# A token-mixing, attention and expert tower: rebuilt prologue and epilogue

## Chip, cores and metric

The kernel runs on one core of a Trainium2 chip. The metric is the device time of one execution in microseconds (us).

## What is computed

The input is x of 64 samples, 128 rows and 192 values. The reference, cut to what matters:

```python
def tok(x):                                   # per sample: 128 channels, 64 x 3 pixels
    h = layernorm(x.reshape(b, t, 192), ln0_g, ln0_b)
    h = relu(conv2d(h, conv1_w, conv1_b, ((2, 2), (1, 1))))       # 5 x 3 taps, 128 -> 128
    h = layernorm(h, ln0_g, ln0_b)
    h = relu(conv2d(h, conv2_w, conv2_b, ((2, 2), (0, 0))))       # 5 x 2 taps, 128 -> 128
    h = layernorm(h, ln1_g, ln1_b)
    h = relu(conv2d(h, conv3_w, conv3_b, ((2, 2), (0, 0))))       # 5 x 2 taps, 128 -> 256
    res = layernorm(concat(two halves), ln1_g, ln1_b)
    return res @ out_w + out_b                                    # 128 tokens of width 64
def attn(x):
    q, vf, vb = split(x @ wqv_w.T + wqv_b)                        # 8 heads of width 64
    a = -sum_w |q[s] - k[t]| / 8, k = x * wk                      # L1 distance, all pairs of tokens
    a = softmax(concat(a, 0), axis=s)[:t]
    o = sum over heads of (a @ vf + a.T @ vb)
    return x + (o * sigmoid(1.702 * o)) @ fanin_w.T + fanin_b
def ffn(x):                                   # one expert of 32 for each token
    idx = argmax(x @ router_w.T + router_b)
    return relu(relu(x @ W1[idx] + b1[idx]) @ W2[idx] + b2[idx])
h = tok(x); h = h + attn(norm(h)); h = h + ffn(norm(h))
```

## The kernel before

The work goes by pairs of samples, 32 pairs in all. For each pair there are four stages: `tok` (the three convolutions and their layer norms), `norm` and `kq` (the norm ahead of attention, the keys `kT` and the queries `qparts`), the 128 **units** with `attend`, and `experts`. A unit is one head with 16 query tokens of one sample: TensorE makes the differences q - k of all its pairs in PSUM with four bf16 matmuls (line 403), and one engine takes the absolute value and adds. For a unit that is not *shared* VectorE does both in one reduction (line 805, about 1.2 us). For a *shared* unit ScalarE writes the absolute values to `absd` (line 601, about 1.0 us), then a DMA adds the two halves of a group of two to four units (line 1061), GpSimd adds three more levels (lines 1072 to 1079), and VectorE finishes with a short reduction (line 816). The table `SHARED` (line 45) says for each of the 16 groups of 8 slots which heads are shared. The unit in slot s uses place s mod 3 of the PSUM tensor `psU`, so TensorE waits for the reader of slot s - 3.

All engines run the same list of 128 slots for each pair, each engine its own part, and each engine carries out its instructions in the order in which they are written. The tables `AT_AT`, `EX_AT`, `NORM_AT`, `KQ_AT` and `TOK_AT` (lines 126 to 135) say at which slot a step is written. Iteration i holds the units of pair i, the second half of `attend` and the `experts` of pair i - 1, `norm` and `kq` of pair i + 1 and `tok` of pair i + 2. So the **prologue** must do `tok` of pairs 0 and 1 and `norm` and `kq` of pair 0 before the first unit, and the **epilogue** has the second half of `attend` and the `experts` of the last pair, for which no other work is left.

In the prologue SP issues the loads in one row: x of pair 0, the list `first` (`ident`, `ln0g`, `ln0b`, `w1`, `b1`), then `weights`, `parts_of` and at last x of pair 1. All engines wait for the whole of `first`, and from the second layer on for the whole of the rest (semaphore `loaded`; VectorE waits for it at the slot of conv1, lines 1018 to 1020, and then runs `weigh`, which makes the table `pattern` from the key weights). Then all engines go through 256 slots with pair 0 at slot s and pair 1 at s - 40:

```python
for s in range(2 * SLOTS):
    tok(0, s, psL, lead_pe, lead_act, lead_dve)
    norm(0, s - SLOTS)
    kq(0, 0, s - SLOTS - QUERY_AFTER)      # QUERY_AFTER = 66
    tok(1, s - LEAD)                       # LEAD = 40
```

SP then loads `flat` from `pattern` (four DMAs of 768 KB) and, once `qpart3` is made, from the queries; unit 0 waits for these and for `kT`. The convolutions and most small matmuls are in f32 and appear in the trace as two records each. In the epilogue every step of `attend` and `experts` goes through the one PSUM bank `psZ`: `turna` and `turnb` (the attention weights transposed, four heads each), `pv` (eight matmuls), `fan`, `turn`, `route`, `turnoh`, `hida`, `hidb` (the experts' hidden layer in two halves) and `out`, each of which waits until the one before has been read.

Of the kernel before, what the change touches and what calls it, by code (L numbers as in the profile page):

```python
# [25 lines left out]
T = 128  # L26
J = 64
# [28 lines left out]
LEAD = 40  # L56
QUERY_AFTER = 66
# [7 lines left out]
def group_ends(slot):  # L65

    return 0 <= slot < SLOTS and slot % HEADS == SHARED[slot // HEADS][-1]
# [69 lines left out]

def vit_tower(nc, a, out):
    PAIRS = a["x"].shape[0] // 2
    x_v = a["x"].rearrange("b t f -> t b f")  # L140
    out_v = out.rearrange("b t w -> t b w")

    with ExitStack() as ctx:  # L143
# [3 lines left out]
        def sem(name):  # L147
# [30 lines left out]
        one = sb("one", [T, 1])  # L178

# [62 lines left out]
        loaded_first = sem("loaded_first")  # L242
        loaded = sem("loaded")
        ready = sem("ready")
        filled = sem("filled")
# [22 lines left out]
        first = [(ident, a["ident"]), (ln0g, a["ln0g"]), (ln0b, a["ln0b"]), (w1, a["w1"]), (b1, a["b1"])]  # L268
        weights = [
            (w2, a["w2"]), (b2, a["b2"]), (ln1g, a["ln1g"]), (ln1b, a["ln1b"]), (w3, a["w3"]), (b3, a["b3"]),  # L270
            (ln1g_col, a["ln1g_col"]), (ln1b_col, a["ln1b_col"]), (wout, a["wout"]), (bout, a["bout"]),
            (wk, a["wk"]), (rank, a["rank"]), (we2, a["we2"]),
# [5 lines left out]
        READY = 18  # L278
        FIRST = 16 * len(first)
# [15 lines left out]
        def _(sp):  # L295
            sp.dma_start(xin[:, :, :], x_v[:, 0:2, :]).then_inc(x_in, 16)
            for dst, src in first:
                sp.dma_start(dst[:], src).then_inc(loaded_first, 16)
            for dst, src in weights:
                sp.dma_start(dst[:], src).then_inc(loaded, 16)  # L300
            sp.wait_ge(zeroed, 1)
            for dst, src in parts_of:
                sp.dma_start(dst, src).then_inc(loaded, 16)
# [20 lines left out]
            def prologue():  # L324
                load_x(1)
                load_x(2)
                sp.wait_ge(pattern_made, 14)
# [36 lines left out]
        def _(pe):  # L364
# [8 lines left out]
            def unit(i, slot):  # L373
# [21 lines left out]
                if isinstance(j, int) and j < 0:  # L395
                    pass
                elif shared(before):
                    pe.wait_ge(a_abs, A_PAIR * j + A_BEFORE[before + 1])
                else:
                    pe.wait_ge(d_done, D_PAIR * j + D_BEFORE[before + 1])  # L400
# [76 lines left out]
            def attend(p, b, slot):  # L477
# [11 lines left out]
                for n, name in enumerate(("turna", "turnb")):  # L489
                    for m in spread(slot, AT_AT[name], AT_AT["turn_len"], 4):  # L490
                        if m == 0:
                            take_bank(at_act, AT_ACT.after(g, ("turneda", "turnedb")[n]))
                            pe.wait_ge(at_act, AT_ACT.after(g, ("scale3", "scale7")[n]))
                        mm = nc.tensor.transpose(psZ[:, m * T:m * T + T], P[:, 4 * n + m, 0, :], ident[:, :])
# [12 lines left out]
            def experts(p, slot):  # L507
# [23 lines left out]
                for n, name in enumerate(("hida", "hidb")):  # L531
                    for m in spread(slot, EX_AT[name], EX_AT["hid_len"], 2):
                        if m == 0:
                            take_bank(ex_act, EX_ACT.after(p, ("relua", "relub")[n]))
                        q = 2 * n + m
                        mm = nc.tensor.matmul(psZ[:, m * 256:m * 256 + 256], we1[:, q * T:q * T + T], xa[:, :],  # L536
# [3 lines left out]
                for q in spread(slot, EX_AT["out"], EX_AT["out_len"], 5):  # L540
                    if q == 0:
                        take_bank(ex_act, EX_ACT.after(p, "relu"))
                    mm = nc.tensor.matmul(psZ[0:LAT, 0:256], be2[:, :] if q == 4 else we2[:, q, :],  # L543
# [8 lines left out]
            def prologue():  # L552
                pe.wait_ge(loaded_first, FIRST)
                pe.wait_ge(ready, READY)
                for s in range(2 * SLOTS):
                    if s == TOK_AT["conv2"]:
                        pe.wait_ge(loaded, LOADED)
                    tok(0, s, psL, lead_pe, lead_act, lead_dve)
                    norm(0, s - SLOTS)
                    kq(0, 0, s - SLOTS - QUERY_AFTER)  # L560
                    tok(1, s - LEAD)

            def iteration(i, late=True, tokens=True, ahead=True):
# [3 lines left out]
                for s in range(SLOTS):  # L567
# [23 lines left out]
        def _(act):  # L591
            def unit(i, slot):
                if not shared(slot):
                    return
                c = slot // HEADS
                u = SHARED[c].index(slot % HEADS)
# [100 lines left out]
            def attend(p, b, slot):  # L697
# [6 lines left out]
                for n in spread(slot, AT_AT["exp"], AT_AT["exp_len"], HEADS):  # L704
                    if n == 0:

                        act.wait_ge(d_done, D_PAIR * p + D_BEFORE[64 * (b + 1)])
                        act.wait_ge(a_done, TREES * p + CHUNKS * (b + 1))
# [7 lines left out]
                for n, name in enumerate(("turna", "turnb")):  # L716
                    if slot == AT_AT[name] + AT_AT["turn_len"]:
                        act.wait_ge(at_pe, AT_PE.after(g, name))
                        nc.scalar.activation(P[:, 4 * n:4 * n + 4, 1, :],  # L719
                                             psZ[:, :].rearrange("p (h t) -> p h t", h=4), ACT.Copy).then_inc(at_act, 1)  # L720
# [11 lines left out]
            def experts(p, slot):  # L732
# [501 lines left out]
```

## Time and profile before

| | |
|---|---|
| three runs | 3576.53, 3578.32, 3587.60 us; median 3578.32 us |
| profiled execution | 3586.24 us, of which the span from first to last instruction 3584.1 us |
| busy in the span | TensorE matmuls 3276.2 us (91%), VectorE 3115.8 (87%), GpSimd 2851.3 (80%), ScalarE 2694.5 (75%) |
| first unit starts | 82.8 us |
| last units end | 3534.5 us |
| the softmax of the last half pair starts | 3547.1 us |
| mean granted TensorE clock | 0.983 |

"Span" is read from the profile's first line; the rest of the profiled time (2.1 us) lies outside it. A window row gives for each engine its busy time and its count of instructions in a stretch. A timeline row gives start, duration, engine, line, operation, output and inputs, and in brackets how long the engine was idle before it and what it waited for.

### The profile page before, as it was taken

How to read it: one execution, taken by the hardware profiler on the slowest of the kernel's cores; microseconds unless marked ns; L12 is line 12 of the kernel's file. 1: busy time of each engine (PE TensorE's matmuls, PEld its weight loads, DVE VectorE, ACT ScalarE, POOL GpSimd, SP SyncE). 2: the span in 40 equal slices, each digit the busy share in tenths (PEclk: the TensorE clock that was granted, in tenths of full speed). 3: DMA queues.
4: the chain of work that ended last, by engine and by line, in shares of the span. 5: the costliest groups of instructions: out<-in, count | busy, mean ns of one | idle time of the engine just before them, and what ended most of it. 6: DMA issues, size and time to landing. Idle time of an engine off the chain costs nothing. (4 is left out here: it accounts for less than half of the span.)

```text
span 3584.1 us, 78481 instructions
## 1 busy us (share of the span) xinstructions
PE 3276.2 (91%) x23008; PEld 2420.3 (68%) x23008; DVE 3115.8 (87%) x4449; ACT 2694.5 (75%) x4801; POOL 2851.3 (80%) x2724
## 2 busy tenths in 40 slices
PE   5899999999999999999999999999999999999886
PEld 4666667666667766667666677666677666677554
DVE  3889988898898898888899899899899899898884
ACT  1777877777877777777777777777777777777774
POOL 1788888888888888878888888888888888888874
PEclk8999999999999999999999999999999999999998
DMA  3777877787777787777887777787877787777874
GB/s 94 154 157 153 161 151 154 150 165 154 156 153 156 153 162 156 155 148 151 158 160 155 157 153 154 157 158 155 159 153 155 156 158 155 155 153 152 160 157 82
DMA packets 198692, 545.31 MB, mean 152 GB/s; under 512 B 68054, under 2 KB 132438, under 8 KB 145272
## 3 DMA queue, kind: packets, MB, share of 16 engines
q0 software_dynamic: 73728, 503.35, 71.0%
q1 hardware_dynamic: 124920, 41.40, 5.9%
q8 instruction: 24, 0.39, 0.0%
q14 instruction: 20, 0.16, 0.0%
HBM read 10.79 MB, written 2.10 MB: 4 GB/s over the span
## 5 line engine op out<-in xcount | busy, mean ns | idle before, releaser
L805 DVE TENSOR_REDUCE S<-psU 128x16 f32<-128x1024 f32 x2176 | 2603.5, 1217 | 295.7 <-PE psU L403 288.4
L403 PE MATMUL psU<-flat,kT 99*128 99x256 bf16 x16384 | 2315.7, 275 | 230.5 <-ACT absd L601 106.6
L601 ACT ACTIVATE absd<-psU 128x1024 f32<-128x1024 f32 x1920 | 1957.8, 1023 | 627.0 <-PE psU L403 604.7
L403 PEld LDWEIGHTS psU<-flat,kT 99*128 99x128 bf16 x16384 | 1489.2, 98 | 915.2 <-DVE S L805 235.7
L1072 POOL TENSOR_TENSOR absd<-absd 128x1024 f32<-128x1024 f32 (+2 forms) x512 | 1182.1, 2309 | 195.3 <-DMA absd<-absd 194.3
L1061 POOL DMA_DIRECT2D absd<-absd x512 | 453.9, 886 | 297.6 <-ACT absd L601 254.5
L1076 POOL TENSOR_TENSOR absd<-absd 128x512 f32<-128x512 f32 (+2 forms) x512 | 611.0, 1193 | 40.2
L1079 POOL TENSOR_TENSOR absd<-absd 128x256 f32<-128x256 f32 (+2 forms) x512 | 352.4, 688 | 40.1
L415 PE MATMUL psC<-c1in,w 128*128 128x384 f32 (+1 forms) x930 | 315.1, 421 | 0.6
L501 PE MATMUL psZ<-P,v 128*128 128x256 f32 x1024 | 311.2, 386 | 0.8 <-ACT P L719 0.8
L434 PE MATMUL psC<-c3in,w 128*128 128x128 f32 x1240 | 255.6, 289 | 4.5 <-DVE c3in L847 4.2
L816 DVE TENSOR_REDUCE S<-absd 128x64 f32<-128x256 f32 (+2 forms) x512 | 201.5, 393 | 34.8 <-POOL absd L1079 33.0
L434 PEld LDWEIGHTS psC<-c3in,w 128*128 128x128 f32 x1240 | 195.6, 193 | 37.0 <-issue 25.6
L423 PE MATMUL psC<-c2in,w 128*128 128x256 f32 x620 | 186.6, 383 | 1.5 <-DVE c2in L847 1.5
L715 ACT ACTIVATE P<-P,rden 128x128 f32<-128x128 f32 x512 | 175.0, 393 | 0.3 <-DVE rden L919 0.3
L501 PEld LDWEIGHTS psZ<-P,v 128*128 128x128 f32 x1024 | 156.1, 192 | 16.6 <-ACT P L719 7.8
L710 ACT ACTIVATE P<-S 128x129 f32<-128x129 f32 x512 | 152.9, 305 | 10.6 <-DVE S L816 10.6
L415 PEld LDWEIGHTS psC<-c1in,w 128*128 128x128 f32 x930 | 141.7, 191 | 9.9 <-DVE c1in L847 4.3
L485 PE MATMUL psZ<-wqv,x1T_late 65*128 65x256 f32 x512 | 135.0, 386 | 0.7 <-ACT v L702 0.7
L1138 POOL TENSOR_TENSOR qparts<-qrest,qparts 128x512 bf16<-128x512 f32 x64 | 83.5, 1304 | 25.3 <-ACT qparts L695 25.3
L710 ACT ACTIVATION_READ_ACCUMULATOR P<-S 128x1 f32 x512 | 99.8, 195 | 0.0
L423 PEld LDWEIGHTS psC<-c2in,w 128*128 128x128 f32 x620 | 93.7, 190 | 5.5 <-DVE c2in L847 2.0
(166 smaller groups left out, 2187.0 us busy)
## 6 DMA issues: line engine op xcount, KB each, us to landing
absd<-absd POOLq DMA_DIRECT2D x416, 1024.0 KB, 7.8
flat<-qparts SPq DMA_DIRECT2D x3072, 8.0 KB, 4.0
absd<-absd POOLq DMA_DIRECT2D x64, 768.0 KB, 6.5
absd<-absd POOLq DMA_DIRECT2D x32, 512.0 KB, 4.8
xin<-in_x SPq DMA_DIRECT2D x32, 192.0 KB, 7.9
flat<-pattern SPq DMA_DIRECT2D x4, 768.0 KB, 10.8
out_h<-result SPq DMA_DIRECT2D x32, 64.0 KB, 5.9
w<-in_w SPq DMA_DIRECT2D x1, 1280.0 KB
```

The costliest lines, as they stand in the source:

```text
L403: mm = nc.tensor.matmul(psU[:, slot % PLACES, m], kT[0:ROWS + 3, b, m, :], flat[0:ROWS + 3, half % HALVES, :, lo:lo + BLOCK], start=True, ...
L415: mm = nc.tensor.matmul(o_v[:, :, :, o:o + wn], w1[:, 3 * dy + dx, :], c1in[:, :, dy:dy + J, w0:w0 + wn], start=(n == 0), stop=(n == 14))
L423: mm = nc.tensor.matmul(z[:, 0:4 * J].rearrange("p (b j w) -> p b j w", b=2, w=2), w2[:, n, :], c2in[:, :, dy:dy + J, dx:dx + 2], start=(n ...
L434: mm = nc.tensor.matmul(z[:, 0:2 * T].rearrange("p (b a j) -> p b a j", b=2, a=2)[:, :, hf, :], w3[:, m, hf * T:hf * T + T], c3in[:, :, dy ...
L501: mm = nc.tensor.matmul(psZ[:, 0:2 * T], v[:, n, :, :].rearrange("p a w -> p (a w)"), P[:, n, :, :].rearrange("p a t -> p (a t)"), start=( ...
L601: nc.scalar.activation(absd[:, c % GROUPS, :, u], psU[:, slot % PLACES].rearrange("p (n a) s w -> p n (a s w)", n=2), ACT.Abs).then_inc(a_ ...
L710: nc.scalar.activation(P[:, n, :, :].rearrange("p a t -> p (a t)")[:, 0:T + 1], S[:, b, n, :], ACT.Exp, scale=-1.0 / 8.0, accum_out=den[:, ...
L805: nc.vector.tensor_reduce(S[:, b, hd, SB * c:SB * c + SB], psU[:, slot % PLACES].rearrange("p a s w -> p s a w"), AX.XY, ALU.add, apply_ab ...
L1061: nc.gpsimd.dma_start(absd[:, c % GROUPS, 0, 0:n], absd[:, c % GROUPS, 1, 0:n], accum_op=ALU.add) \
L1072: nc.gpsimd.tensor_tensor(lo, lo, hi, ALU.add).then_inc(a_tree, 1)
L1076: nc.gpsimd.tensor_tensor(lo, lo, hi, ALU.add).then_inc(a_tree, 1)
L1079: nc.gpsimd.tensor_tensor(lo, lo, hi, ALU.add).then_inc(a_tree, 1)
```

## The change

- **Loads.** `first` is cut into `for_norm` (`ln0g`, `ln0b`), `for_conv1` (`w1`, `b1`) and `for_keys` (`ident`, `wk`), with a semaphore each; then x of pair 1, then `for_conv2`, then the rest. Each step waits for its own part only.
- **Constants.** Those that the first layer doesn't need are set behind the first layer norm (semaphore `ones`); four small ones go to GpSimd. ScalarE runs a one-column Copy at the start. `weigh` is cut in two, `split_keys` and `weigh`, and put behind pair 0's first and second layer norm.
- **Order.** The two loops of 256 slots give way to `lead_in`: a table of how far pair 0 and pair 1 have got at each step. Pair 0's queries are made in the middle of pair 1's conv3, its keys behind pair 1's last layer norm; pair 1's last three slots are written in slot 0 of iteration 0 (`lead_out`).
- **Matmuls on zeros.** 44 bf16 matmuls of 256 columns at the start (`WARM`), and in the epilogue 50, 16, 31, 9, 14 and 2 ahead of `turna`, `fan`, `turn`, `route`, `turnoh` and `hida` (`STILL`). Their output is overwritten or not read.
- **Last pair.** `SHARED_LAST` takes the place of `SHARED` in the last four groups of the last pair: 9 shared units there in place of 15. `turnb` and `hidb` go to the bank `psC`, so that `pv` can begin when the first four heads are ready and `hidb` need not wait for the reader of `hida`.

```diff
+SHARED_LAST = {12: (1, 5), 13: (2, 4, 6), 14: (1, 5), 15: (0, 2)}
...
+LEAD_IN = [(43, 31), (46, 31), (48, 36), (59, 36), (63, 37), (73, 49), (75, 50), (76, 51), (77, 54), (116, 74),
+           (117, 74), (127, 78), (128, 89), (128, 92)]
+LEAD_LAST = (95, 118, 125)
+LEAD_TAIL = 1
+WEIGH = (2, 3)
+WARM = 44
+
+def lead_in(first, second, norm, kq, between=None):
+    n, k = NORM_AT, KQ_AT
+    now = [0, 0]
+    def run(job, *slots):
+        for x in dict.fromkeys(slots):
+            job(x)
+    def run_to(row, first_to, second_to):
+        run(first, *range(now[0], first_to))
+        run(second, *range(now[1], second_to))
+        now[:] = first_to, second_to
+        if between:
+            between(row)
+    for row, (first_to, second_to) in enumerate(LEAD_IN):
+        run_to(row, first_to, second_to)
+    run(norm, n["stat"], n["rstd"], n["x"])
+    run_to(-1, SLOTS, LEAD_LAST[0])
+    run(norm, n["turn"], n["turn"] + 1)
+    run(kq, *range(k["q"], k["q"] + max(k["q_len"], 1)), k["qpart1"], k["qrest1"], k["qpart2"], k["qpart3"])
+    run_to(-1, SLOTS, LEAD_LAST[1])
+    run(norm, n["part1"], n["rest1"], n["part2"], n["part3"], n["hx"])
+    run(kq, k["kT"], k["kT"] + 1)
+    run_to(-1, SLOTS, LEAD_LAST[2])
+
+def lead_out(second, slot):
+    for x in spread(slot, 0, LEAD_TAIL, SLOTS - LEAD_LAST[2]):
+        second(LEAD_LAST[2] + x)
+
+STILL = dict(turna=50, fan=16, turn=31, route=9, turnoh=14, hida=2)
...
+        for_norm = [(ln0g, a["ln0g"]), (ln0b, a["ln0b"])]
+        for_conv1 = [(w1, a["w1"]), (b1, a["b1"])]
+        for_keys = [(ident, a["ident"]), (wk, a["wk"])]
+        for_conv2 = [(w2, a["w2"]), (b2, a["b2"]), (ln1g, a["ln1g"]), (ln1b, a["ln1b"])]
...
# TensorE
             def prologue():
-                pe.wait_ge(loaded_first, FIRST)
-                pe.wait_ge(ready, READY)
-                for s in range(2 * SLOTS):
+                pe.wait_ge(stilled, 1)
+                for n in range(WARM):
+                    nc.tensor.matmul(psU[:, 0, 0], still[:, 0:T], still[:, :], start=True, stop=True)
...
+            def stay_awake(n):
+                for _ in range(n):
+                    nc.tensor.matmul(psU[:, 125 % PLACES, 0], still[:, 0:T], still[:, :], start=True, stop=True)
             def epilogue():
+                pe.wait_ge(d_done, d_before(PAIRS - 1, 126))
                 for s in range(SLOTS):
-                    attend(PAIRS - 1, 1, s)
-                    experts(PAIRS - 1, s)
+                    for name, n in STILL.items():
+                        if s == (EX_AT[name] if name in EX_AT else AT_AT[name]):
+                            stay_awake(n)
+                    attend(PAIRS - 1, 1, s, psC)
+                    experts(PAIRS - 1, s, psC)
...
# TensorE, pv: the second four heads wait for turnb's copy on their own
+                        pe.wait_ge(at_act, AT_ACT.after(g, "turnedb" if other is None else "turneda"))
+                    if n == HEADS // 2 and other is not None:
                         pe.wait_ge(at_act, AT_ACT.after(g, "turnedb"))
...
# ScalarE
             def prologue():
+                act.wait_ge(stilled, 1)
+                nc.scalar.activation(still_act[:, :], still[:, 0:1], ACT.Copy).then_inc(stilled, 1)
...
# VectorE
+                def between(row):
+                    if row == WEIGH[0]:
+                        split_keys()
+                    if row == WEIGH[1]:
+                        weigh()
...
# every engine, iteration 0 only
+                    if not late:
+                        lead_out(lambda x: tok(1, x), s)
```

## Rows read from the trace of the kernel before

**Rows 1.** Windows, instructions of line 415: busy (count) of PE, PEld; clock; DMA share; GB/s.

```profile
14.70:18.10 3.40, 3.39 (x7) 2.43 (x8) 1.00 0.99 206
18.10:25.00 6.90, 6.86 (x24) 4.58 (x23) 1.00 0.30 71
```

**Rows 2.** Timeline of the prologue's first layer, all engines.

```profile
9.44 0.23 DVE L980 CAST ident_b<-ident 128x128 bf16<-128x128 f32 x1 [3.37 <-DMA b<-in_b]
...
11.03 0.49 ACT L610 ACTIVATE psU<-xin 128x384 f32<-128x384 f32 x1
...
14.71 10.26 PE L415 MATMUL psU<-c1in,w 128*128 128x384 f32 x30 [14.71 <-DVE c1in L847]
...
22.18 0.18 DVE L984 TENSOR_REDUCE pick<-ident 96x1 f32<-96x32 f32 x1 [7.62 <-DMA be<-in_be]
...
31.33 5.94 PE L423 MATMUL psU<-c2in,w 128*128 128x256 f32 x14 [6.37 <-DVE c2in L847]
```

**Rows 3.** Timeline: from one convolution to the next, and conv3's pace.

```profile
47.33 0.56 ACT L614 ACTIVATE psC<-psC,b 128x384 f32<-128x384 f32 x1 [6.70 <-PE psC L415]
...
50.87 1.13 PE L423 MATMUL psC<-c2in,w 128*128 128x256 f32 x4 [1.49 <-DVE c2in L847]
...
63.83 3.36 PE L434 MATMUL psC<-c3in,w 128*128 128x128 f32 x26
```

**Rows 4.** Timeline: from pair 0's tokens to the first units.

```profile
64.07 0.29 DVE L895 TENSOR_TENSOR h<-psU,bout 128x128 f32<-128x128 f32 x1 [3.25 <-PE psU L447]
...
66.77 0.77 ACT L642 ACTIVATE x<-h,nmrn,rstdn 128x64 f32<-128x64 f32 x2 [3.90 <-POOL nmrn L1100]
...
72.04 0.55 ACT L661 ACTIVATE x1T<-psZ 64x128 f32<-64x128 f32 x2
...
75.16 0.60 ACT L692 ACTIVATE qparts<-psZ 128x512 bf16<-128x512 f32 x1 [2.56 <-PE psZ L472]
...
78.42 1.15 POOL L1138 TENSOR_TENSOR qparts<-qrest,qparts 128x512 bf16<-128x512 f32 x1 [6.63 <-ACT qparts L695]
...
82.83 6.15 PE L403 MATMUL psU<-flat,kT 99*128 99x256 bf16 x32 [5.64 <-DMA flat<-qparts]
```

**Rows 5.** Windows, last 32 units, line 805: busy (count) of DVE; clock; DMA share; GB/s.

```profile
3510.60:3534.50 23.90, 20.64 (x18) 1.00 0.77 151
```

**Rows 6.** Windows, the same stretch: PE, PEld, DVE, ACT, POOL; clock; DMA; GB/s.

```profile
3510.60:3534.50 23.90, 20.96 (x152) 14.51 (x149) 22.10 (x25) 18.66 (x29) 18.23 (x16) 1.00 0.77 151
```

**Rows 7.** Timeline: the last units, the last group, the softmax.

```profile
3532.09 2.39 DVE L805 TENSOR_REDUCE S<-psU 128x16 f32<-128x1024 f32 x2
...
3542.08 2.34 POOL L1072 TENSOR_TENSOR absd<-absd 128x1024 f32<-128x1024 f32 x1 [2.55 <-DMA absd<-absd]
...
3547.09 0.31 ACT L710 ACTIVATE P<-S 128x129 f32<-128x129 f32 x1 [10.56 <-DVE S L816]
```

**Rows 8.** Page, DMA issues: count, KB each, us to landing.

```profile
absd<-absd POOLq DMA_DIRECT2D x32, 512.0 KB, 4.8
```

**Rows 9.** Timeline: one loop-time matmul group, then the epilogue's.

```profile
3488.66 1.13 PE L485 MATMUL psZ<-wqv,x1T_late 65*128 65x256 f32 x4
...
3551.24 1.08 PE L494 MATMUL psZ<-ident,P 128*128 128x128 f32 x4 [15.34 <-ACT P L715]
...
3554.90 5.88 PE L501 MATMUL psZ<-P,v 128*128 128x256 f32 x16 [0.78 <-ACT P L719]
...
3560.82 0.27 ACT L725 ACTIVATE o_half<-psZ 64x128 f32<-64x128 f32 x1 [6.06 <-PE psZ L501]
...
3571.49 2.08 PE L536 MATMUL psZ<-xa,we 128*128 128x256 f32 x4 [0.95 <-ACT ohT L746]
...
3580.78 0.56 ACT L756 ACTIVATE fT<-psZ 64x128 f32<-64x128 f32 x2 [3.82 <-PE psZ L543]
```

**Rows 10.** Timeline of DVE: tokens of pairs 3 and 31.

```profile
302.55 0.28 DVE L895 TENSOR_TENSOR h<-psC,bout 128x128 f32<-128x128 f32 x1
3323.57 0.28 DVE L895 TENSOR_TENSOR h<-psC,bout 128x128 f32<-128x128 f32 x1
```

More of the change, by code:

```diff
@@ L141, in vit_tower, with last, heads_of, is_shared @@
     out_v = out.rearrange("b t w -> t b w")
+    def last(i):
+        return isinstance(i, int) and i == PAIRS - 1
+    def heads_of(i, c):
+        return SHARED_LAST.get(c, SHARED[c]) if last(i) else SHARED[c]
+    def is_shared(i, slot):
+        return slot % HEADS in heads_of(i, slot // HEADS)
+    def group_ends(i, slot):
+        return 0 <= slot < SLOTS and slot % HEADS == max(heads_of(i, slot // HEADS), default=-1)
+    def a_before(i, slot):
+        return A_PAIR * i + (sum(is_shared(i, x) for x in range(slot)) if last(i) else A_BEFORE[slot])
+    def d_before(i, slot):
+        return D_PAIR * i + (sum(not is_shared(i, x) for x in range(slot)) if last(i) else D_BEFORE[slot])
+    def groups_before(i, c):
+        return TREES * i + (sum(len(heads_of(i, x)) > 0 for x in range(c)) if last(i) else c)
     with ExitStack() as ctx:
@@ L178, in vit_tower @@
         one = sb("one", [T, 1])
+        still = sb("still", [T, 2 * T], BF16)
+        still_act = sb("still_act", [T, 1])
         xin = sb("xin", [T, 2, 3 * J])
@@ L542, in experts @@
                         take_bank(ex_act, EX_ACT.after(p, "relu"))
+                    if q == 2 and other is not None:
+                        pe.wait_ge(ex_act, EX_ACT.after(p, "relub"))
                     mm = nc.tensor.matmul(psZ[0:LAT, 0:256], be2[:, :] if q == 4 else we2[:, q, :],
@@ L592, in unit @@
             def unit(i, slot):
-                if not shared(slot):
+                if not is_shared(i, slot):
                     return
                 c = slot // HEADS
-                u = SHARED[c].index(slot % HEADS)
+                u = heads_of(i, c).index(slot % HEADS)
                 act.wait_ge(made, SLOTS * i + slot + 1)
@@ L759, in prologue, with first @@
             def prologue():
-                act.wait_ge(loaded_first, FIRST)
-                act.wait_ge(ready, READY)
-                for s in range(2 * SLOTS):
+                act.wait_ge(stilled, 1)
+                nc.scalar.activation(still_act[:, :], still[:, 0:1], ACT.Copy).then_inc(stilled, 1)
+                def first(s):
+                    if s == TOK_AT["conv1"]:
+                        act.wait_ge(loaded_conv1, 16 * len(for_conv1))
                     if s == TOK_AT["conv2"]:
+                        act.wait_ge(loaded_conv2, 16 * len(for_conv2))
+                        act.wait_ge(ones, ONES)
+                    if s == TOK_AT["conv3"]:
                         act.wait_ge(loaded, LOADED)
                     tok(0, s, psL, lead_pe, lead_act, lead_dve)
-                    norm(0, s - SLOTS)
-                    kq(0, 0, s - SLOTS - QUERY_AFTER)
-                    tok(1, s - LEAD)
+                lead_in(first, lambda s: tok(1, s), lambda s: norm(0, s), lambda s: kq(0, 0, s))
             def iteration(i, late=True, tokens=True, ahead=True):
@@ L783, in iteration @@
                         kq(i + 1, 0, s - SECOND)
+                    if not late:
+                        lead_out(lambda x: tok(1, x), s)
                     if tokens:
@@ L797, in unit @@
             def unit(i, slot):
-                if shared(slot):
+                if is_shared(i, slot):
                     return
@@ L867, in tok @@
                 if slot == TOK_AT["a"] + TOK_AT["gap"]:
-                    lead("conv1")
-                    affine("a", ln0g, ln0b, c1in, 3 * J, q, z, by_dve, by_pool)
+                    affine("a", ln0g, ln0b, c1in, 3 * J, q, z, by_dve, by_pool, lead)
                 if slot == TOK_AT["b"]:
@@ L873, in tok @@
                 if slot == TOK_AT["b"] + TOK_AT["gap"]:
-                    lead("conv2")
-                    affine("b", ln0g, ln0b, c2in, 3 * J, q, z, by_dve, by_pool)
+                    affine("b", ln0g, ln0b, c2in, 3 * J, q, z, by_dve, by_pool, lead)
                 if slot == TOK_AT["c"]:
@@ L1038, in iteration @@
                         kq(i + 1, 0, s - SECOND)
+                    if not late:
+                        lead_out(lambda x: tok(1, x), s)
                     if tokens:
@@ L1146, in prologue, with first @@
             def prologue():
+                for t, value in ((small, EPS), (half, -0.5), (minus, -1.0), (one, 1.0)):
+                    nc.gpsimd.memset(t[:, :], value).then_inc(ready, 1)
                 pool.wait_ge(ready, READY)
-                for s in range(2 * SLOTS):
+                def first(s):
                     tok(0, s, lead_dve, lead_pool)
-                    norm(0, s - SLOTS)
-                    kq(0, 0, s - SLOTS - QUERY_AFTER)
-                    tok(1, s - LEAD)
+                lead_in(first, lambda s: tok(1, s), lambda s: norm(0, s), lambda s: kq(0, 0, s))
             def iteration(i, late=True, tokens=True, ahead=True):
@@ L1163, in iteration @@
                         kq(i + 1, 0, s - SECOND)
+                    if not late:
+                        lead_out(lambda x: tok(1, x), s)
                     if tokens:
```

178 lines of the change are left out of this document (97 added, 81 removed).

## The prediction

> **What bounds the kernel now.** I read the slices of the page first: VectorE and TensorE are busy at a level over the whole loop, and the slices fall off only at both ends. The loop is not changed: its pace is (3323.57 - 302.55) / 28 = 107.9 us for a pair [rows 10]. So the case is about two stretches: the 82.8 us before the first unit [rows 4], and the 49.6 us from the end of the last unit, 3532.09 + 2.39 = 3534.5 [rows 7], to the end of the span at 3584.1. I read both in the timeline, and the end in the chain of waits too.
>
> In the first stretch the reader is to see four things. ScalarE takes x only at 11.03, since it waits for the cast that waits for the last of `first`, `b1`, which is there at 9.44 [rows 2]. conv1 of pair 0 holds TensorE from 14.71 to 24.97. VectorE stands still until 22.18 for the last of all loads and then does `weigh` ahead of the second layer norm, so that conv2 starts at 31.33 [rows 2]. And pair 0's queries, whose input is normed at 66.77 + 0.77 = 67.5, are first copied at 75.16 and leave GpSimd at 79.57 [rows 4], because they are written behind all of pair 1. In the last stretch nothing runs from 3534.5 to 3547.09 but the last group's DMA and GpSimd adds [rows 7]; from there on each step waits for the one before, on TensorE often at half pace.
>
> **The start, up to conv1.** ScalarE no longer waits for the loads' end; x, `ln0g` and `ln0b` come first, so the first layer norm, 14.71 - 11.03 = 3.7 us long [rows 2], is done well before `b1` lands. `b1` has one load fewer ahead of it: 0.5 us before 9.44, so conv1 begins at 8.9 (bounds: 7.6, the end of the zeros, and 9.4, if order changes nothing). conv1 itself: in its first 3.4 us TensorE did 7 records, 0.48 us each, later 24 in 6.86 us, 0.286 each [rows 1]. The clock column says 1.00 for both, but the first pace is that of 1.2 GHz. With the zeros ahead I take all 30 at about 0.25, between half of 0.48 and 0.286: 7.6 us instead of 10.26. The 44 zeros are bf16 with 256 columns like the units' matmuls, of which 32 took 6.15 us at low pace [rows 4], 0.19 each; half of a little over 0.2, or 0.107, is my price at 2.4 GHz. With some 3.4 us at the low pace as conv1 had it they last 6.4 us from 1.2 on, and are over at 7.6. conv1 of pair 0 ends at 16.5 instead of 24.97.
>
> The Trainium skill ("TensorE: Matmul & The Clock Gate", Part 1) says that throttled is the default state and that activity releases it, which is what the counts of records show and the clock column doesn't. Were the column right, the zeros at the start would be worth nothing and the sum 2.6 us smaller.
>
> **The middle.** `c1in` is shared, so pair 1's shift (0.7) follows conv1's end; then 22 records of pair 1's conv1 stand ahead of pair 0's conv2 in TensorE's queue: 16.5 + 0.8 + 22 x 0.25 = 22.8. Pair 0's second norm needs 50.87 - 47.33 = 3.5 us [rows 3] plus some 2 us for `split_keys` between its statistics and its gain on VectorE: ready at about 22, hidden under TensorE by under 1 us. conv2: 20 records x 0.21 = 4.3, to 27.1. `weigh` (4 us) lies behind the norm under conv2. Next norm 3.5, to 30.6; all loads are in by about 22 [rows 2], so none is waited for. conv3: 40 x 3.36 / 26 = 5.2 [rows 3], to 35.8; then pair 1's conv2, 4.3, to 40.1, and its norm, 3.5, to 43.5. Pair 0's last norm, turn and `out` run beside these, but its add (`h`) stands on VectorE behind pair 1's third norm: 43.5.
>
> **Queries and keys.** From `h` to `x1` 2.7 and 0.8 [rows 4]: 47.0. Transposition 0.4, copy 0.55, q matmuls 1.1 (the loop's four records of that shape [rows 9]): 49.1. Before, 4.4 us lay between the first copy's start and GpSimd's end, of which 0.60 and 1.15 are shown [rows 4] and two steps of about 0.65 lie between; the rest was keys and waits. Now 0.6 + 0.65 + 0.65 + 1.15 = 3.1, to 52.2. `flat` landed 82.83 - 79.57 = 3.3 after that, so 55.5. The keys are what is late next: they are moved behind pair 1's last norm, whose GpSimd root stands behind `qpart3`; root, two splits, transposition and copy come to 4.1 us, 0.8 more than the loads (bounds 0 and 2). First unit at 56.3. `lead_out` puts pair 1's `out` and add into slot 0, where VectorE waits for them before its first unit: 0.9 back (bounds 0 and 2). Prologue: 82.8 - 56.3 - 0.9 = **25.6 us** less. Each chained step hides a wait of a tenth or two that I can't see, 5 in all at most; conv1's start gives 1.4 either way.
>
> **The last pair.** In the last 32 units VectorE worked 22.1 of 23.9 us [rows 6], 20.64 of it units [rows 5], 17 whole ones at 1.2. It gets 6 more: 7.2 us, 29.3 in all, and with 1.2 of idle left 30.5: the units end 6.6 later (5.4 if all idle is filled, 9 if runs of VectorE units leave TensorE waiting). Against that stands the wait of 12.6 us behind them. The last group is now two units, whose slot (122) is followed by five VectorE units; its DMA starts about 5.2 us before the units' end and lands after 4.8 [rows 8], then GpSimd needs 2.5 (half the operands of a group that begins with 2.34 [rows 7], plus the fixed part) and VectorE 0.3: softmax at 2.3 after the units' end (0.1 to 5). Gain 12.6 - 2.3 - 6.6 = **3.7 us**.
>
> **The tail.** The 50 zeros start after `vf` and `vb`, about 0.5 after the units' end, and last 50 x 0.107 = 5.4 at 2.4 GHz: they end at 5.9, while `turna` can start at 2.3 + 4.15 = 6.4 [rows 7, 9]. Then `turna` to `o_half` took 9.58 [rows 9]. Now TensorE is at full pace, 16 records of `pv` take 3.4 instead of 5.88, and `pv` starts behind `turna`'s copy, 1.8 after `turna`: 5.4, a gain of 4.2. `fan`: 16 zeros (1.7) against a wait of 1.35, a loss of 0.3. `turn`, `route`, `turnoh`: each faster by 0.2 to 0.45, held up by 0 to 0.3: +0.3. `hida` to `fT` took 9.29; now four records 1.1 (as in the loop, against 2.08 [rows 9]), `hidb` at once behind, ScalarE's copy 0.6, and `out` starts on the first half: 4.1, a gain of 5.2. Together **9.4 us** (6 to 11).
>
> **Sum.** 25.6 + 3.7 + 9.4 = 38.7: 3586.2 - 38.7 = 3547.5 for the profiled execution. That one lies 7.9 above the median of the runs shown, and the gain doesn't depend on it: 3578.3 - 38.7 = **3539.6 us**. A measurement can tell 0.3% (11 us) from no change.
>
> **Rivals.**
> - *The zeros don't raise the clock*, at the start and in the tail. For it: no row shows a matmul on zeros. Against it: records at full pace follow any dense stretch here. Then conv1 starts behind zeros of twice the length (10.7) at low pace (-4.4), the 122 zeros of the tail take 0.213 each and stand in the way (about -12.7: 5 for `turna`, 2 for `fan`, 3 for `turn`, 3 for the two others), and the tail's gain of 9.4 shrinks to 4, by the second bank. Left: 38.7 - 4.4 - 12.7 - 5.4 = 16: 3562.
> - *VectorE's queue sets the prologue.* Both halves of `weigh` cost 5.8 us on its path before (22.18 to 27.98, where the statistics start). If both delay a norm that TensorE waits for, about 6 us of the gain go; with each handover a little late, 10: 3550.
> - *The units end much later.* If the six moved units cost 9 and the softmax still waits 5, the last pair loses 1.4 instead of gaining 3.7: 3545. This lies in the range.
> - *Slower than before: the loop falls into another step.* The order in the loop hangs together by semaphores, and the prologue hands it another start: pair 1's tokens come late into iteration 0. If that shift lasted and each of 31 pairs took 38.7 / 31 = 1.25 us more than 107.9, nothing would be left, and above that the kernel is slower; at 2 us it stands at 3602. Against it: the unit pace is bound by VectorE in all slices alike, after the low-clock stretches as well.
> - *More than said*: conv1 from 7.5 on, keys in time, no wait for `lead_out`, tail 11: 3534 to 3530.
>
> **Chances.** Forecast, 3530 to 3550: 0.66 (the body of it 3533 to 3547). Zeros without effect: 0.10. VectorE's queue: 0.12. More than said: 0.06. The loop in another step: 0.06, half of it slower than before. Between 3524 and 3557 lies what leaves out the zeros' rival and the loop's. Faster 0.93, same 0.04, slower 0.03.
>
> **What would show it.** In the profile after: conv1's 30 records from about 8.9 in about 7.6 us; conv2 of pair 0 at about 23; `h` of pair 0 at 43 to 44 with VectorE busy ahead of it; first unit at 56 to 57, released by `kT`; the six units more on line 805 and the softmax 2 to 3 us behind the last of them; zeros at 0.107 us each in the tail; `pv` in 3.4; `hida` to `fT` about 4. The prediction is wrong if zeros run at 0.213 in the tail, if the first unit starts after 62, or if the pace of the loop leaves 107.9 by more than 0.3.

## Result, and the profile after

The changed kernel takes 3562.35 us (median of 8 runs, 3552.77 to 3578.06), the kernel before 3579.84 us in the same session (8 runs, 3571.75 to 3587.60). The ratio is 0.9951, 95% interval 0.9930 to 0.9972: 17.5 us faster, where 38.7 were forecast, and above the upper end of the range (3557).

The profiled execution of the changed kernel took 3552.77 us. It is the fastest of the eight, while that of before lies 6.4 us above its median, so the two profiles differ by 33.1 us of span and the medians by 17.5. The start, in the timeline:

```profile
1.07 6.61 PE L642 MATMUL psU<-still 128*128 128x256 bf16 x44 [1.07 <-DVE still L1075]
8.62 7.82 PE L493 MATMUL psU<-c1in,w 128*128 128x384 f32 x30 [0.94 <-DMA b<-in_b]
23.00 4.49 PE L501 MATMUL psU<-c2in,w 128*128 128x256 f32 x20
43.17 0.28 DVE L1007 TENSOR_TENSOR h<-psU,bout 128x128 f32<-128x128 f32 x1
50.96 1.15 POOL L1259 TENSOR_TENSOR qparts<-qrest,qparts 128x512 bf16<-128x512 f32 x1 [5.14 <-ACT qparts L800]
55.31 0.59 ACT L789 ACTIVATE kT<-psZ 96x512 bf16<-96x512 bf16 x1 [1.08 <-PE psZ L542]
56.01 1.01 PE L481 MATMUL psU<-flat,kT 99*128 99x256 bf16 x4 [0.50 <-ACT kT L789]
```

conv1 (8.62) waits for `b1` alone; its 30 records take 7.8 us where they took 10.26. The queries leave GpSimd at 52.1 instead of 79.57, the keys are what comes last, and the first unit starts at 56.0 instead of 82.83 [rows 4].

The end, in the timeline of the same execution (the answers to [rows 5, 7, 9]):

```profile
3515.77 3.47 DVE L918 TENSOR_REDUCE S<-psU 128x16 f32<-128x1024 f32 x3
3517.03 2.07 PE L563 MATMUL psZ<-wqv,x1T_late 65*128 65x256 f32 x4 [0.71 <-DVE S L918]
3521.48 0.28 DVE L929 TENSOR_REDUCE S<-absd 128x32 f32<-128x128 f32 x1 [1.78 <-POOL absd L1200]
3521.66 6.57 PE L681 MATMUL psU<-still 128*128 128x256 bf16 x50
3522.40 0.30 ACT L815 ACTIVATE P<-S 128x129 f32<-128x129 f32 x1
3528.07 0.60 PE L576 MATMUL psZ<-ident,P 128*128 128x128 f32 x4
3529.45 3.69 PE L585 MATMUL psZ<-P,v 128*128 128x256 f32 x16 [0.34 <-ACT P L824]
3543.29 1.13 PE L621 MATMUL psZ<-xa,we 128*128 128x256 f32 x4 [0.73 <-ACT ohT L852]
3547.63 0.56 ACT L862 ACTIVATE fT<-psZ 64x128 f32<-64x128 f32 x2 [1.70 <-PE psZ L630]
```

The last units end at 3519.2, the softmax starts 3.2 us behind them and not 12.6, `pv` takes 3.7 instead of 5.88, and `hida` to `fT` 4.3 instead of 9.29.

Between start and end lies the loop. The same two adds that gave its pace before [rows 10], the tokens of pairs 3 and 31, in the timeline after:

```profile
274.25 0.28 DVE L1007 TENSOR_TENSOR h<-psC,bout 128x128 f32<-128x128 f32 x1
3303.71 0.28 DVE L1007 TENSOR_TENSOR h<-psC,bout 128x128 f32<-128x128 f32 x1
```

That is 3029.5 us for the 28 pairs, against 3021.0 before. The whole account, with what I had for each part:

| stretch | before | after | difference | forecast |
|---|---|---|---|---|
| to the first unit | 82.8 | 56.0 | -26.8 | -26.5 |
| from there to `h` of pair 3 | 219.7 | 218.2 | -1.5 | +0.9 |
| `h` of pair 3 to `h` of pair 31 | 3021.0 | 3029.5 | **+8.4** | **0** |
| from there to the end | 260.5 | 247.3 | -13.2 | -13.1 |
| span | 3584.1 | 3551.0 | -33.1 | -38.7 |

The sums of both ends came out as forecast. What is missing is in the loop, of which the change touches no instruction: 8.4 us in this execution, while the medians fall some 21 us short of the forecast.

### The profile page after: what moved, and what is told of

It is laid out like the page before. It is cut to its first block and busy times, and to the rows that moved or that the text cites. A ratio compares the mean times of both kernels' runs of the same rounds, so it can differ in the third digit from the quotient of the medians.

```text
span 3551.0 us, 78815 instructions
## 1 busy us (share of the span) xinstructions
PE 3291.4 (93%) x23174; PEld 2433.9 (69%) x23174; DVE 3124.4 (88%) x4452; ACT 2691.1 (76%) x4796; POOL 2845.6 (80%) x2728
## 5 line engine op out<-in xcount | busy, mean ns | idle before, releaser
L918 DVE TENSOR_REDUCE S<-psU 128x16 f32<-128x1024 f32 x2182 | 2612.0, 1218 | 284.3 <-PE psU L481 276.1
L706 ACT ACTIVATE absd<-psU 128x1024 f32<-128x1024 f32 x1914 | 1953.0, 1024 | 626.8 <-PE psU L481 602.4
L929 DVE TENSOR_REDUCE S<-absd 128x64 f32<-128x256 f32 (+2 forms) x512 | 201.4, 394 | 31.3 <-POOL absd L1200 30.1
L563 PEld LDWEIGHTS psZ<-wqv,x1T_late 65*128 65x128 f32 x512 | 87.9, 192 | 14.3 <-ACT v L807 1.4
```

The costliest lines, as they stand in the source:

```text
L563: mm = nc.tensor.matmul(psZ[:, m * HALF:m * HALF + HALF], x1T_late[0:65, b * T:b * T + T], wqv[0:65, lo:lo + HALF], start=True, stop=True)
L706: nc.scalar.activation(absd[:, c % GROUPS, :, u], psU[:, slot % PLACES].rearrange("p (n a) s w -> p n (a s w)", n=2), ACT.Abs).then_inc(a_ ...
L918: nc.vector.tensor_reduce(S[:, b, hd, SB * c:SB * c + SB], psU[:, slot % PLACES].rearrange("p a s w -> p s a w"), AX.XY, ALU.add, apply_ab ...
```

## Experiments

Ratios are to runs of the kernel before in the same session, with 95% intervals. Its median was 3579.84 in the first session (e1 to e4), 3582.43 in the second (e5 to e8), 3583.18 in the third (e9 to e12), 3582.89 in the fourth (e13 to e16) and 3579.83 in the last (e17, e18).

### The parts alone

**e1**: the changed kernel once more, for a second profile. **e2**: the prologue alone; the epilogue is that of before:

```diff
-SHARED_LAST = {12: (1, 5), 13: (2, 4, 6), 14: (1, 5), 15: (0, 2)}
+SHARED_LAST = {}
-STILL = dict(turna=50, fan=16, turn=31, route=9, turnoh=14, hida=2)
+STILL = dict()
...
-                    attend(PAIRS - 1, 1, s, psC)
-                    experts(PAIRS - 1, s, psC)
+                    attend(PAIRS - 1, 1, s)
+                    experts(PAIRS - 1, s)
```

**e3**: the epilogue alone, with loads, constants and prologue of before. **e4**: the changed kernel without its matmuls on zeros:

```diff
-WARM = 44
+WARM = 0
-STILL = dict(turna=50, fan=16, turn=31, route=9, turnoh=14, hida=2)
+STILL = dict()
```

> The changed kernel once more, for a second trace and more times. In its profiled execution the first unit starts 26.8 us earlier than before and the stretch behind pair 31's tokens is 13.2 us shorter, together 40.0, but the loop between took 7 us more, and the median of the runs gained only 17.5. Theory A (the stretches outside the loop are fixed, and the loop's length varies from run to run with how often TensorE's clock falls in it): first unit again at 56.0, the stretch behind pair 31's tokens again 247 us, and the difference of this run's span to 3551 lies wholly in the loop, with the low clock's time. If A is all, the ratio to before over many runs is 0.989. Theory B (the changed kernel's loop is systematically longer, by some 20 us in the median, through something that the change moved): ratio again 0.995.

> The new prologue (loads, order, 44 matmuls on zeros) with the epilogue, the shared units and the single bank of before. Theory A: 26.8 us less, ratio 0.9925. Theory B1 (the new prologue is what lengthens the loop): about 5 us less, ratio 0.9985. Theory B2 (the epilogue's zeros or the tensor for them lengthen it): as A or between.

> The new epilogue (nine shared units in place of fifteen in the last four groups, the second bank, the zeros) with the prologue of before. Theory A: 13.2 us less, ratio 0.9963. Theory B1 (the prologue lengthens the loop): also 13.2 less. Theory B2 (it is the epilogue's side or the added tensor): no gain or a loss, ratio 1.000 to 1.002.

> The changed kernel without any matmul on zeros. If the zeros hold the clock up at both ends as said, conv1 of pair 0 takes 10.3 us again in place of 7.8 (first unit 1 to 3 us later), and the tail from turna to o_half and from hida to fT loses together 3 to 5 us: 4 to 8 us slower than the changed kernel. A rival: the zeros cost the loop something (a clock that falls later instead), then it is as fast or faster, ratio to before 0.99.

| | median us | ratio | first unit at | `h` of pair 3 to 31 |
|---|---|---|---|---|
| e1 changed kernel again | 3564.56 | 0.9948 (0.9929 to 0.9968) | 56.0 | 3037.8 |
| e2 prologue alone | 3575.77 | 0.9982 (0.9970 to 0.9995) | 56.8 | 3034.2 |
| e3 epilogue alone | 3586.00 | 1.0022 (1.0009 to 1.0036) | 80.6 | 3035.4 |
| e4 without zeros | 3566.83 | 0.9966 (0.9951 to 0.9980) | 57.8 | 3028.4 |

The timeline of e1 has the same two adds, 3037.8 us apart:

```profile
280.28 0.28 DVE L1007 TENSOR_TENSOR h<-psC,bout 128x128 f32<-128x128 f32 x1
3318.05 0.28 DVE L1007 TENSOR_TENSOR h<-psC,bout 128x128 f32<-128x128 f32 x1
```

Two things follow. First, the parts do not add up. The prologue alone starts its units 26 us earlier and gains 6.4 us by the ratio; the epilogue alone shortens its end (from the first unit of pair 31) from 155.3 to 144.4 us and *loses* 7.9; both together gain about 18. Each part loses some 20 us, and both together lose them only once. In all four traces the loop is longer than the 3021.0 us of the kernel before. So the loss belongs to something that all four kernels share, and not to the prologue's order or to a state that it hands to the loop.

Second, the zeros do what I said, for little. In e4's timeline:

```profile
8.19 10.12 PE L493 MATMUL psU<-c1in,w 128*128 128x384 f32 x30 [8.19 <-DMA b<-in_b]
3531.62 1.09 PE L576 MATMUL psZ<-ident,P 128*128 128x128 f32 x4 [5.83 <-ACT P L820]
3533.67 4.50 PE L585 MATMUL psZ<-P,v 128*128 128x256 f32 x16
```

Without zeros conv1 takes 10.1 us instead of 7.8, `turna` 1.09 instead of 0.60 and `pv` 4.5 instead of 3.7. From the softmax to the end it is 30.8 us against 28.6. So the zeros are worth 1.8 us at the start and 2.2 at the end, 4.0 in all. The times agree only roughly: e4's median is 2.3 above that of e1 in the same session, by the ratios it is 6.4, and the intervals of the two overlap. That settles the rival of zeros without effect, whose 3562 is by chance the measured time: later zeros run at 0.11 us each (31 in 3.55).

### What all four share: two tensors ahead of the others

The change declares `still` (512 bytes for each partition) and `still_act` (4 bytes, rounded up to 32) ahead of `xin`, so that every later tensor starts 544 bytes higher in SBUF. **e5** puts the two unused tensors into the kernel before; **e6** moves them behind the last tensor of the changed kernel; **e7** and **e8** put one unused tensor of 32 or of 512 bytes into the kernel before, in the same place.

```diff
# e5, kernel before
+        still = sb("still", [T, 2 * T], BF16)
+        still_act = sb("still_act", [T, 1])
         xin = ...
# e6, changed kernel
-        still = sb("still", [T, 2 * T], BF16)
-        still_act = sb("still_act", [T, 1])
         xin = ...
         result = sb("result", [T, 2, LAT])
+        still = sb("still", [T, 2 * T], BF16)
+        still_act = sb("still_act", [T, 1])
# e7, kernel before (e8: 128 elements instead of 8)
+        gap = sb("gap", [T, 8])
```

> The kernel before with nothing but the two added tensors, still and still_act, declared where the changed kernel has them and never used. They shift every tensor behind them by 544 bytes, so that flat, qparts and absd no longer start at a multiple of 64 bytes. Theory L (the place of the tensors in memory lengthens the loop): about 20 us more, ratio 1.0055, with the 512-byte packets of the query loads slower as in all kernels with the added tensors (39.0 ns for 37.7). Theory C (something in the changed code does it): ratio 1.000.

> The changed kernel with still and still_act declared behind all other tensors, so that all others lie where they lay before. Theory L: the loop as before, the whole 40 us gained, ratio 0.989, packets of 512 bytes 37.7 ns. Theory C: ratio 0.995 as the changed kernel.

> The kernel before with one unused tensor of 32 bytes per partition ahead of xin. Theory L with the alignment to 64 bytes as its cause: as much slower as with the two tensors, ratio 1.005. If the cause is a longer shift (another place in memory, not the alignment): ratio 1.000.

> The kernel before with one unused tensor of 512 bytes per partition ahead of xin, which keeps each tensor's place modulo 64. Theory L with the alignment as its cause: ratio 1.000. If it is the place itself: 1.005.

| | median us | ratio |
|---|---|---|
| e5 before, with the two tensors unused | 3594.42 | 1.0036 (1.0024 to 1.0047) |
| e6 changed kernel, the two tensors last | 3546.85 | 0.9899 (0.9884 to 0.9913) |
| e7 before, 32 bytes more | 3599.85 | 1.0042 (1.0028 to 1.0057) |
| e8 before, 512 bytes more | 3582.36 | 1.0001 (0.9990 to 1.0013) |

It is the placement. Two tensors that nothing reads slow the kernel before by 0.4%. 512 bytes do nothing, 32 bytes do it all: what counts is where a tensor starts within 512 bytes, and within 256 by e15 below, which moves the large tensors by 256 and costs nothing. With the same instructions and the tensors moved back, the change gains 35.6 us, 3 less than forecast. The changed kernel and e6 were not measured in one session, but the intervals of their ratios (0.9930 to 0.9972 and 0.9884 to 0.9913) lie apart.

### Which tensors, and what they gain at 256

Counted from their shapes, with each tensor rounded up to 32 bytes, `qrest`, `qparts`, `flat`, `absd` and `S` start 192 bytes past a multiple of 256 before and 224 bytes past one in the changed kernel; `xin` to `kT` go from 32 past a multiple of 64 to a multiple of 64 (`c2in` the other way). Gaps of unused bytes move each group by itself. e9 to e11 have 32 bytes on either side of one tensor, which puts what follows it at a multiple of 256:

```diff
# e9, kernel before (e10: around qparts, e11: around absd)
+        gap_a = sb("gap_a", [T, 8])
         flat = ...
+        gap_b = sb("gap_b", [T, 8])
# e12, e6 with 32 bytes ahead of xin and 32 ahead of qrest
# e13, kernel before, 32 bytes ahead of qrest (e14: 64)
+        gap_b = sb("gap_b", [T, 8])
         qrest = sb("qrest", [T, HW])
# e15, kernel before, 32 bytes ahead of xin and 224 ahead of qrest (e16: 32 and 32)
# e17, kernel before, 32 bytes ahead of P; e18: 32 ahead of qrest and 32 ahead of P
```

> The kernel before with 32 unused bytes ahead of flat and 32 behind it, so that of the large tensors flat alone starts off a multiple of 64 bytes. Theory F (the query loads write flat more slowly, and the units wait for it): ratio 1.004 and the 512-byte packets at 39 ns. If it is qparts or absd: 1.000, packets at 37.7 ns for absd.

> The same with the 32 bytes around qparts, the source of the query loads. Theory F: 1.000. Theory Q (reading off the multiple is what is slow): 1.004 and packets at 39 ns.

> The same with the 32 bytes around absd, which the adding DMAs read and write and three engines use. Theories F and Q: 1.000, packets of 512 bytes at 37.7 ns. Theory D (the adding DMAs or GpSimd's adds are slower there): 1.004.

> The changed kernel with its two tensors last and 32 unused bytes ahead of xin and again ahead of qrest, so that the tensors from xin to kT, which lie at 32 modulo 64 in the kernel before, also start at a multiple of 64. If only the query loads matter: ratio 0.990 to before, as with the tensors last alone. If each tensor gains by it: 0.986 to 0.989.

> The kernel before with 32 unused bytes ahead of qrest: qrest, qparts, flat, absd and S start 32 bytes off a multiple of 64 (224 past a multiple of 256), everything ahead of them stays. If the tensors of the loop are what counts together, this repeats the shift of everything: 1.004 of the time before (about 3597 us), and the query loads' 512-byte packets take 39 ns instead of 37.7. If the small tensors ahead of them carry it, 1.000.

> The kernel before with 64 unused bytes ahead of qrest: qrest, qparts, flat, absd and S all start at a multiple of 256 bytes, everything ahead of them stays. If the transfers' placement is the whole cause, the loop loses some 20 us: 0.9945 (3561 us), 512-byte packets at 31 ns. With absd and flat at 256 alone the kernel before had 0.996, so that is the nearest bound for a smaller effect; 1.000 if the small tensors carried the gain of the changed kernel's best placement.

> The kernel before with 32 unused bytes ahead of xin and 224 ahead of qrest: xin to kT start at a multiple of 64 instead of 32 past one, the loop's large tensors stay 192 past a multiple of 256. If the large tensors carry both effects: 1.000. If the small ones carry the loss seen with the shift of everything: 1.004.

> The kernel before with 32 unused bytes ahead of xin and 32 ahead of qrest: small tensors at multiples of 64, large ones at multiples of 256, the placement of the fastest version so far. That version is 54 us under the kernel before; 38.7 was my forecast for the change itself, so the placement alone should give 15 to 21 us here: 0.9945 to 0.996 (3562 to 3567 us), the same as with the large tensors alone moved.

> The kernel before with 32 unused bytes ahead of P: P, v and everything behind them start 32 bytes off a multiple of 64, qrest to S stay 192 past a multiple of 256. If the transfers' tensors carry the loss: 1.000 (3583 us). If it is P, v and the engines' small tensors: 1.004 to 1.007.

> The kernel before with 32 unused bytes ahead of qrest and 32 ahead of P: qrest, qparts, flat, absd and S start 32 bytes off a multiple of 64, P and what is behind it at a multiple of 64 as before. If the transfers' tensors carry the loss: 1.004 to 1.007 (3597 to 3608 us), the wait of POOL's first add for the adding transfers at 205 to 211 us instead of 194. Otherwise 1.000.

The columns of tensors give the start past a multiple of 256 bytes. "Packet" is the mean time of the trace's 512-byte packets, of which nine in ten belong to the query loads. "V waits" is VectorE's wait for GpSimd's shared units between 83 and 3480 us, and "low" the time between the first units of pairs 0 and 31 with the granted clock at its low level, both in the profiled execution.

| | `qparts` | `flat` | `absd` | ratio | packet ns | V waits us | low us |
|---|---|---|---|---|---|---|---|
| before | 192 | 192 | 192 | 1 | 37.7 | 19.6 | 56 |
| e15 (`xin` to `kT` moved) | 192 | 192 | 192 | 0.9995 (0.9983 to 1.0007) | 37.6 | 18.0 | 55 |
| e17 (`P` and later moved) | 192 | 192 | 192 | 0.9996 (0.9987 to 1.0006) | 37.5 | 19.3 | 54 |
| e13 (from `qrest` on) | 224 | 224 | 224 | 1.0069 (1.0049 to 1.0088) | 39.2 | 30.5 | 45 |
| e18 (`qrest` to `S`) | 224 | 224 | 224 | 1.0049 (1.0035 to 1.0063) | 39.3 | 33.2 | 91 |
| e9 | 192 | 224 | 0 | 0.9997 (0.9986 to 1.0008) | 37.5 | 15.9 | 52 |
| e10 | 224 | 0 | 0 | 0.9962 (0.9948 to 0.9976) | 37.2 | 11.1 | 58 |
| e11 | 192 | 192 | 224 | 0.9994 (0.9983 to 1.0005) | 37.7 | 20.4 | 77 |
| e14 (from `qrest` on) | 0 | 0 | 0 | 0.9976 (0.9965 to 0.9986) | 31.8 | 14.6 | 55 |
| e16 (e14, `xin` to `kT` too) | 0 | 0 | 0 | 0.9968 (0.9958 to 0.9979) | 31.6 | 16.2 | 53 |
| changed kernel | 224 | 224 | 224 | 0.9951 (0.9930 to 0.9972) | 39.0 | 27.9 | 68 |
| e6 (changed) | 192 | 192 | 192 | 0.9899 (0.9884 to 0.9913) | 37.7 | 24.0 | 68 |
| e12 (changed) | 0 | 0 | 0 | 0.9859 (0.9842 to 0.9876) | 31.3 | 12.6 | 31 |

e15 and e17 clear the small tensors on both sides, e13 and e18 convict the group `qrest` to `S`. Within it no tensor alone repeats the loss: `absd` alone at 224 costs nothing (e11), and in e9 and e10 `absd` had moved to 0 along with the one put off. The gain at 0 was about half of what I expected for e14 (0.9945) and less than for e16 (0.9945 to 0.996). e12 is the fastest version, 3529.0 us: 54 us under the kernel before and 33 under the changed one.

How the placement reaches the time can be read in the chain behind a transfer. The page's issues and queues give the transfers, first in the changed kernel,

```profile
q1 hardware_dynamic: 124920, 41.40, 6.1%
...
flat<-qparts SPq DMA_DIRECT2D x3072, 8.0 KB, 4.0
absd<-absd POOLq DMA_DIRECT2D x64, 768.0 KB, 6.7
```

then in e12:

```profile
q1 hardware_dynamic: 124920, 41.40, 5.4%
...
flat<-qparts SPq DMA_DIRECT2D x3072, 8.0 KB, 3.6
absd<-absd POOLq DMA_DIRECT2D x64, 768.0 KB, 6.3
```

The same packets and bytes take less of the engines' time, and land 0.4 us earlier. From 192 to 224, the step that the change made, the page shows less: 4.0 and 6.5 us in the kernel before, 4.0 and 6.7 in the changed one. The next link is GpSimd, which begins a group's adds when the adding transfer has landed. The waits over the whole span (engine, line, waited for; us, times, longest) in the kernel before, in e18 and in e14:

```profile
POOL absd L1072 <- DMA absd<-absd: 194.3, 276, 3.1
```

```profile
POOL absd L1074 <- DMA absd<-absd: 209.3, 273, 3.1
```

```profile
POOL absd L1073 <- DMA absd<-absd: 128.9, 227, 3.0
```

This wait costs nothing by itself, since GpSimd has time to spare. The last link has none: VectorE carries out its list in order, and where a group is not ready the units behind it stand. Its waits between 83 and 3480 us in the same three kernels:

```profile
DVE S L816 <- POOL absd L1079: 19.6, 38, 2.3
```

```profile
DVE S L818 <- POOL absd L1081: 33.2, 60, 2.5
```

```profile
DVE S L817 <- POOL absd L1080: 14.6, 19, 2.3
```

In the kernels with the instructions of before this wait follows the placement: 18.0 to 20.4 us with all three tensors at 192 or `absd` alone off (before, e8, e11, e15, e17), 27.1 to 33.2 with all at 224 (e5, e7, e13, e18), 11.1 to 16.2 with `absd` at 0 (e9, e10, e14, e16). The changed kernel, e6 and e12 stand in the same order: 27.9, 24.0, 12.6. At 224 that is 7 to 14 us more on the engine that sets the pace, of a loss of 12 to 25 us. The two adds that bound the loop, in e18's timeline,

```profile
298.83 0.28 DVE L897 TENSOR_TENSOR h<-psC,bout 128x128 f32<-128x128 f32 x1
3342.64 0.28 DVE L897 TENSOR_TENSOR h<-psC,bout 128x128 f32<-128x128 f32 x1
```

are 3043.8 us apart, 22.8 more than before. The engines' instructions take as long as before (in e18 and before, on average: a unit's reduction on VectorE 1218 and 1217 ns, its absolute values on ScalarE 1024 and 1023, GpSimd's first add 2306 and 2309). What grew is VectorE's idle time between the two adds, from 302 to 321 us, and the wait for GpSimd is 13.6 us of that. Nor is this wait the whole of the time: e9 waits as little as e14 and e16 (15.9 us against 14.6 and 16.2), but it is no faster than the kernel before, and they are by 0.2 to 0.3%.

Another part goes with the granted clock. All runs have theirs on record: among the runs of the kernel before, in each of the five sessions, one with a mean clock 0.001 higher was about 2 us shorter (1.7 to 2.3). The four kernels with all three at 224 had mean clocks of 0.9797 (e5), 0.9785 (e7), 0.9777 (e13) and 0.9800 (e18), where the kernel before had 0.9823 to 0.9828 in their sessions. By that slope 5 to 9 us of each one's loss go with the clock, as an estimate. A single profiled run does not tell this: e18 has 91 us at the low level against 56 before, e13, of which the fastest of six runs was profiled, 45. Whether the slower transfers cause the drops of the clock is not shown.

## Why the prediction was wrong

**The step that failed** is a sentence of the first paragraph: "The loop is not changed: its pace is ... 107.9 us for a pair". Not one instruction of the loop is changed, but the places of nearly all their operands in SBUF are: the two tensors stand in the diff, in the list of tensors ahead of `xin`, and I costed them at nothing. They cost 12 to 25 us (e5 12.0, e7 17.4, e13 18 to 25, e18 19 by their sessions; the changed kernel against e6 19 by the ratios), about half of what the two ends gained. The profiled execution shows only 8.4 of it, e1 16.8.

**The rival of the loop in another step** named the right place with the wrong cause. It had the new start of the loop as its mechanism. e3 keeps the old prologue and loses all the same, and e6 has the new one and loses next to nothing (0.9899 against the forecast's 0.9892). I gave it 0.06; its check, "if the pace of the loop leaves 107.9 by more than 0.3", is just met by the profile (3029.5 / 28 = 108.2) and clearly by e1 (108.5).

**The start** was right by its steps: conv1 8.9 forecast and 8.62 measured, its length 7.6 and 7.8, conv2 22.8 and 23.0, `h` 43.5 and 43.2, the queries' end 52.2 and 52.1, first unit 56.3 and 56.0, released by `kT`. `lead_out` cost nothing visible: the stretch to `h` of pair 3 became 1.5 shorter where I had 0.9 more. The rival of VectorE's queue did not happen. The 26.8 us are on the high side, though: the kernel before and its twelve variants with unused bytes start their units at 79.8 to 82.8 us, and the one profiled for the comparison is the latest; the variants of the new prologue with zeros start them at 56.0 to 57.3.

**The last pair** gained 4.8, not 3.7. The units end 4.6 later against pair 31's `h` (3519.2 - 3303.7 = 215.5, before 210.9; forecast 6.6), and the softmax is 3.2 behind them and not 2.3. Two errors, in opposite directions.

**The tail** gained 8.4, not 9.4 (37.0 to 28.6 from the softmax on). The mis-sized term is the 50 zeros ahead of `turna`. I had `vf` and `vb` done and the zeros under way 0.5 us after the units' end; in the timeline `vf` and `vb` run at the low pace, 2.07 us for four records, and the zeros last from 3521.66 to 3528.23, 6.6 us and not 5.4. By my 4.15 us from the softmax `turna` could have started at 3526.55; it started at 3528.07. So the zeros hold `turna` up by 1.5 us (by 1.1 in e12, where `vf` and `vb` run at the full pace but the 50 zeros last 7.3), and their net worth in the whole tail is 2.2. Most of the tail's gain comes without them, from the second bank: 37.0 to 30.8 in e4, where my rival left 4 of 9.4.

**The sum** for a kernel with its tensors where they were: -35.6 us measured in e6, -38.7 forecast.

**What stays open.** That it is the tensors from `qrest` to `S` together is shown; which of them, or which pair, is not. `flat` is the likeliest: of e9 and e10, both with `absd` at 0, the one with `flat` at 0 gains 0.4% and the one with `flat` at 224 nothing. The landing of the query loads points the same way: 3.6 us in all kernels with `flat` at 0, 3.8 in e9 and 4.0 or 4.1 in all others. `flat` alone at 224 with `absd` at 192 was not tried. In e5, e7, e13 and e18 the growth of the wait for GpSimd and the clock's estimated share come to 17, 15, 20 and 19 us, about as much as the losses (12, 17, 18 and 19 in the median); the two may overlap, and the wait is from one execution each. Why the clock is lower there, and why e9 gains nothing from its shorter wait, is open.

## What to carry to other kernels

A diff changes more than the instructions in it. A new tensor moves all that are declared behind it; where transfers within SBUF feed the engine that sets the pace, declare it last, and try the transfers' tensors at multiples of 256 bytes (here another 0.2 to 0.4%, for a few unused bytes). When the parts of a change tried alone each fall short by the same amount and the whole falls short only once, look for what they share, not for how they act on each other. And measure a small step on medians: two executions of one kernel differed here by as much as the effect, with the mean granted clock at 0.987 in the fastest of eight and 0.979 in the slowest.

## What the runs showed of the hardware

- **The start of a tensor within 256 bytes sets the time of a packet within SBUF.** The 512-byte packets, most of them of the query loads, took 31.3 to 31.8 ns on average with source and destination at a multiple of 256, 37.5 to 37.9 with both 192 past one, 39.0 to 39.3 with both 224 past one. The adding transfers' packets of 8192 bytes took 641 to 643 ns with `absd` at 0, and 657 to 658 at 192 and at 224 alike.

  The Trainium skill ("DMA: Bandwidth & Descriptors", "How a descriptor splits into AXI transactions") says that each transaction must start at a multiple of 256 bytes and that the bytes ahead of an unaligned start still cost beats of 32 bytes. By that rule, and as an estimate from it, 512 bytes are 16, 22 and 23 beats at 0, 192 and 224, and the order and steps of the measured times agree. With one side off they don't: 37.2 ns with the source at 224 and the destination at 0, where 23 beats for the source would mean 39, and 37.5 with 192 and 224.
- **The clock column does not show the first stretch.** The 30 records of conv1 took 10.12 us without zeros ahead and 7.82 with them, and the column reads 1.00 for both. The stretch, its length, TensorE's busy time and records, the granted clock, the transfers' share and GB/s, in e4 and in the changed kernel:

```profile
8.19:18.31 10.12, 10.12 (x30) 1.00 1.03 320
```

```profile
8.62:16.44 7.82, 7.82 (x30) 1.00 1.04 359
```

- **Matmuls on zeros hold TensorE's granted clock up.** From `turna` to the end the granted clock is 1.00 with them and 0.74 without, in the same columns for the changed kernel and for e4:

```profile
3528.07:3551.00 22.93, 18.49 (x128) 1.00 0.02 4
```

```profile
3531.60:3558.30 26.70, 15.62 (x54) 0.74 0.01 3
```

  Still they are worth only 4 us of the 40 that the two ends gained, since the steps they speed up are mostly waits for other engines.
